# In each quarter, the two down products are put ahead of the product that counts choices

## The reference

```python
h = _L0_tok_ref(x, ...)                                   # 8 x 1024 tokens, 512 wide
h = h + _L0_attn_ref(_layernorm(h), ...)                  # 16 heads, causal, distance decay
h = h + _L0_ffn_ref(_layernorm(h), ...)
# in _L0_ffn_ref:
logits = h @ gate_w.T
scores = jnp.sqrt(jax.nn.softplus(logits))
_, topk_idx = jax.lax.top_k(scores + bias[None, :], K)    # K = 6 of 32
topk_w = take(scores, topk_idx); topk_w = 1.5 * topk_w / topk_w.sum(-1)
pos = (cumsum(onehot(topk_idx)) - 1)[topk_idx]            # place in the expert's list, CAP 192
valid = pos < CAP
y = expert(xb)[eid, pos] * w_slot                         # routed part
si = clip(silu(h @ sg.T) * (h @ su.T), -10, 10)
shared = si @ sd.T                                        # shared expert, all tokens
return routed + shared
```

## Time and profile before

| what | us |
|---|---|
| median of 3 runs | 4119.98 |
| lowest and highest of them | 4116.23, 4120.33 |
| the profiled execution, device time | 4117.86 |
| its span in the trace | 4116.0 |
| mean granted clock of TensorE in it, share of full | 0.881 |

### The profile page before, as it was taken

How to read it: one execution, slowest core, us unless ns; L and a number is a source line. 1 busy time by engine, 2 the same in 40 slices (tenths; PEclk the granted TensorE clock), 3 DMA queues, 4 the chain that set the end, 5 groups by cost and what they waited for, 6 DMA issues and landing times. The chain is left out here.

```text
span 4116.0 us, 62979 instructions
## 1 busy us (share of the span) xinstructions
PE 3420.5 (83%) x20360; PEld 1701.3 (41%) x20360; DVE 2504.0 (61%) x6671; ACT 1041.2 (25%) x2427; POOL 1668.7 (41%) x932
## 2 busy tenths in 40 slices
PE   4776569998888998888898989898988987754998
PEld 1222234444444444444444444444444443233776
DVE  3555424655766577567656765776677576643654
ACT  1111103332332233222223322332333222211111
POOL 3223203543544455345444544454455344522233
PEclk6555589999999999999999999999999998876999
DMA  4444210001111110100011010001000100102996
GB/s 155 151 142 170 111 69 1 27 19 34 73 49 65 45 37 12 47 17 32 22 42 42 11 37 27 32 12 42 22 32 11 50 13 21 45 28 78 263 257 162
DMA packets 123186, 257.65 MB, mean 63 GB/s; under 512 B 38988, under 2 KB 39628, under 8 KB 120192
## 3 DMA queue, kind: packets, MB, share of 16 engines
q1 hardware_dynamic: 78832, 204.56, 14.9%
q0 software_dynamic: 44048, 49.26, 4.7%
HBM read 146.71 MB, written 204.26 MB: 85 GB/s over the span
## 5 line engine op out<-in xcount | busy, mean ns | idle before, releaser
L711 POOL TENSOR_TENSOR a_first_probs<-a_first_probs,a_probs 128x2048 f32<-128x2048 f32 (+3 forms) x320 | 1033.2, 3229 | 1595.5 <-ACT a_probs L773 1376.0
L895 DVE CUSTOM_DVE_ANT_0 a_unused<-a_ps_ring,a_decay 128x512 bf16<-128x512 f32 (+3 forms) x1536 | 774.9, 554 | 518.5 <-PE a_ps_ring L1185 510.5
L773 ACT ACTIVATE a_probs<-a_ps_ring 128x512 f32<-128x512 f32 (+3 forms) x1280 | 505.0, 473 | 795.0 <-PE a_ps_ring L1219 600.4
L715 POOL DMA_INDIRECT d_slots<-a_rows,a_place_i x397 | 394.5, 994 | 249.5 <-DVE a_place_i L1047 141.9
L1209 PE MATMUL a_ps_ring<-a_k_t,a_q_t 32*128 32x512 f32 (+3 forms) x3072 | 413.8, 540 | 67.8 <-DVE a_row_max L895 43.5
L1185 PE MATMUL a_ps_ring<-a_q_t,a_k_t 32*128 32x512 f32 (+3 forms) x3072 | 389.4, 541 | 17.3 <-DVE a_row_max L895 12.4
L1281 PE MATMUL a_ps_dense<-a_sd,a_inner_t 128*128 128x512 f32 x256 | 185.2, 863 | 189.4 <-DVE a_gate_up L1027 186.1
L1173 PE MATMUL a_ps_dense<-a_normed_t,a_q_w 128*128 128x512 f32 x512 | 243.4, 619 | 45.0 <-DMA a_normed_t<-d_normed_t 42.4
L1232 PE MATMUL a_ps_heads<-a_probs,a_values 128*32 128x512 f32 (+3 forms) x2560 | 272.4, 500 | 0.0
L1209 PEld LDWEIGHTS a_ps_ring<-a_k_t,a_q_t 32*128 32x128 f32 x3072 | 146.3, 186 | 270.5 <-issue 142.9
L773 ACT ACTIVATE a_first_probs<-a_ps_ring 128x512 f32<-128x512 f32 x256 | 135.6, 604 | 473.2 <-PE a_ps_ring L1219 448.3
(11 more groups left out here) (169 smaller groups left out, 4575.4 us busy)
## 6 DMA issues: line engine op xcount, KB each, us to landing
d_hidden<-e_hidden SPq DMA_DIRECT2D x8, 2048.0 KB, 7.4
d_normed_t<-e_normed_t SPq DMA_DIRECT2D x8, 2048.0 KB, 11.7
a_normed_t<-d_normed_t SPq DMA_DIRECT2D x8, 2048.0 KB, 7.9
a_residual<-d_hidden SPq DMA_DIRECT2D x64, 256.0 KB, 2.7
d_hidden<-a_residual SPq DMA_DIRECT2D x64, 256.0 KB, 2.0
a_hidden<-d_hidden SPq DMA_DIRECT2D x64, 256.0 KB, 2.7
out<-a_hidden SPq DMA_DIRECT2D x64, 256.0 KB, 2.0
x_w_gate<-w_gate SPq DMA_DIRECT2D x32, 512.0 KB, 6.5
```

The lines of the kernel that those rows point to most:

```text
L711: nc.gpsimd.tensor_tensor(total_of, total_of, probs_of(m)[:, :, 0:width], ALU.add).then_inc(added, 1)
L715: nc.gpsimd.indirect_dma_start(slot_rows, bass.IndirectOffsetOnAxis(ap=place_i[p][:, j, choice:choice + 1], axis=0), rows[p][:, j, :], Non ...
L773: nc.scalar.activation(probs_of(m)[:, h, 0:width], score_bank(m, h)[:, 0:width], ACT.Exp).then_inc(exp_done, 1)
L895: nc.vector.tensor_tensor_reduce(unused[:, h, 0:width], row_bank(k, h)[:, 0:width], decay[:, at:at + width], 1.0, NEG, ALU.add, ALU.max, r ...
```

## The change

Two down products of a quarter stand ahead of its place product: down 0 in slot 10 gap C, where place was, down 1 in slot 11 gap A, where down 0 was, and place in slot 11 gap C, where down 1 was. In the epilogue the same table gives PE's order, and the calls of DVE are swapped to match.

```diff
 QUARTER_AT = ((("turn", 0), 4, A), (("turn", 1), 4, B), (("route", 0), 5, C), (("up", 0), 6, C), (("up", 1), 8, C),
-              (("place", 0), 10, C), (("down", 0), 11, A), (("down", 1), 11, C))
+              (("down", 0), 10, C), (("down", 1), 11, A), (("place", 0), 11, C))
...
                 gate(x, 1, epilogue_use(q, "up", 1), chain)
-                find_places(q % 2, epilogue_use(q, "place", 0), chain)
                 for j in range(2):
                     add_shared(j, epilogue_use(q, "down", j))
+                find_places(q % 2, epilogue_use(q, "place", 0), chain)
```

## The result

| what | before | after |
|---|---|---|
| median, us | 4118.1 | 4192.1 |
| lowest and highest | 4107.97, 4120.33 | 4188.84, 4192.69 |
| the profiled execution, device time | 4117.86 | 4191.54 |
| its span | 4116.0 | 4189.7 |

The changed kernel is slower: ratio 1.0182, with a 95% interval of 1.016 to 1.0204. The prediction was 4164, with a range of 4128 to 4202. Of the four runs of after one was disturbed (4499.96): it is counted in the median of 4192.1, which is 4191.5 without it, and neither in the lowest and highest nor in the ratio.

The account below looks back on a forecast made before the run. PE's time was taken as set by DVE's gate up to down 0, then by PE's own work. Quarters +27.7, epilogue +6.2 and clock +10 made +44 on 4117.86, plus 2.1 for the median: 4164, range 4128 to 4202.

Parts of the forecast that it names:

- The two savings: Ahead of down 0: -0.47 without the wait for L1027, and -1.21 in 26 quarters by L919 falling to 0.29.
- the first saving: Down 0 waits only for inner_done, no longer for L1027: -0.47 us a quarter.
- rival 2: L919 ahead of gate stays at 1.5, POOL's addition not being its cause: 31 us come back, 4195; chance 0.12.
- What was added: Start of down 0 to end of scores(0): 11.6 against 8.99, +2.6; with both savings an ordinary quarter +0.9.
- the split: At scores(0), PE does two heads, waits about 0.2 for row_maxima(11), then does the rest: 1.6 with fourth, shift and mask.
- g = 1: Quarter whose next step lacks a dense product in slot 0: wait of 0.2 and split at scores(1), +1.9 in all.
- g = 3: Quarter before the next entry: scores(0) comes 0.97 late anyway, which covers the wait: -0.1.
- second falls: Clock falling again among slot 0 and 1's small products: one quarter in three, +10, between -3 and +45.
- Rival 1: The clock falls again in every quarter, +45 for the clock: 4199; chance 0.13.
- Rival 3: Clock back before down 0, which takes 1.9 not 3.7: 2.2 saved in 26 quarters, 57 in all, 4107; chance 0.07.
- The last four quarters in steps: Of these the last two were put at +2.4 (no saving on L919) and +0.9 (no next step's row scores).
- The epilogue: Three quarters gain 0.46 each; in the last, L1047 and the scatters come 7.6 later: +6.2 in all.

Follow-up runs that it names:

- e2: Kernel before, with POOL's addition L711 of slot 11 made to wait for inner_done so it can't run beside L919: 4093.41, ratio 0.9946.
- e9: Changed kernel with two more useless matmuls of down's shape right ahead of the place product in steps: 4176.14, ratio 1.0135.
- e3: Changed kernel with four more useless matmuls of down's shape right ahead of the place product in steps: 4195.5, ratio 1.0195.
- e1: Changed kernel with place moved between scores(11) and row_scores(11), and down 1 back in front of the next step's scores(0): 4130.95, ratio 1.0042.
- e10: Kernel before in all its steps, with only the epilogue's four quarters in the new order (down 0, down 1, place): 4119.96, ratio 0.9999.
- e5: Changed kernel with six more useless matmuls of down's shape in the wait ahead of down 0: 4134.64, ratio 1.0055.
- e7: Changed kernel with place between scores(11) and row_scores(11), down 1 before scores(0), and six useless matmuls in the wait ahead of down 0: 4077.2, ratio 0.9904.
- e6: Changed kernel with DVE's division of slot 10 behind gate's last step instead of ahead of it: 4143.63, ratio 1.0074.
- e8: Changed kernel with place before row_scores(11), down 1 before scores(0), slot 10's division behind gate, five useless matmuls in down 0's wait: 4040.72, ratio 0.9824.
- e11: Changed kernel with place before row_scores(11), down 1 before scores(0), DVE's division of slot 10 behind gate, no useless work: 4085.47, ratio 0.9929.

## Why the prediction was right and wrong

The direction and the mechanism in a quarter were right, and the time was inside the range; it missed by 28 us. By the estimates of the table the clock cost 53 us and not 10. That the miss is only 28 is in part luck: the rest of the change cost 26 and not 34, and the first quarter happened to come 5.6 earlier.

**The two savings.** The wait on L1027 is gone, and L919 takes 0.29. Down 0 starts 0.05 behind L1062 in after, so the first saving was 0.55 and not 0.47. e2 shows the second by itself, so rival 2 (L919 stays at 1.5) is out. The Trainium skill, "SBUF — State Buffer", section "SBUF: two separate sides", has DVE and GpSimd take the shared ports by an exclusive lock, a DVE operation with two SBUF inputs among them. e2 agrees: the operation beside the addition is slow, whichever it is (L919 1.50 and then 0.29, the old L1029 0.22 and then 1.13). That whoever starts first keeps the ports does not agree with the earlier trace rows, where L919 starts 0.05 before L711 and is the one that waits.

**What was added.** 11.45 for a predicted 11.6, with the wait of 0.31 and the split where they were forecast; for g = 1 the split at `scores(1)` is there too, but the wait ahead of it is put down to ACT (L773) and not to L895. Over 24 quarters the part of the loss that isn't the clock is 66.3 - 48 = 18 by the estimate of the table, for a predicted 12 x 0.9 + 6 x 1.9 - 6 x 0.1 = 21.6. Inside it two steps were off and cancelled: g = 1 was -0.3 in most and not +1.9, g = 0 and g = 2 were +0.5 and not +0.9, and g = 3 was about +1 to +2.6 and not -0.1. Of g = 1 part is the estimate's doing: in the one quarter whose fall came later (16 us behind L1062) it is +1.4, and in the others the slow PE no longer waits the 0.49 that it waited before. The error at g = 3 was a wrong reading of the earlier trace rows, and that row was the longest of five besides. I took the 0.97 of idle time for the lateness of `scores(0)`, but it was only what down 1 left of an edge of the loop that takes 2 to 4 us: 1.9 of down 1 and 0.17 to 0.97, then 3.03 to 3.44 bare, then 1.98 and 0.93 to 1.78 (e9), then 3.70 and mostly nothing (e3).

**The clock, the step that failed.** I put second falls at one in three quarters and 1.7 us each, +10 (by these two numbers it would be +12). They came in two of three (16 of 24), with 3 to 10 us of busy PE at half speed in each: 93.9 - 6.5 = 87.4 us, which cost some 44 by the estimate of the table, and the first falls 4 more. Both the number and the length were too low, because I sized the term by the one fall in the earlier trace rows behind a wait of 0.49, and did not count with about 3 us of idle time at the edge of the loop, where five of the falls are. Rival 1 (a fall in every quarter, 4199) was nearer to the measured time than the forecast, but not by its own count: it had more falls, each as short as the one in the earlier trace rows.

e1, e3 and e9 show that the missing dense product makes the second falls in the stretch: put back, or replaced by useless products in the same place, they go from 12 to 0, 0 and 6 (in all from 16 to 1, 0 and 8), more than the two by which the kernel before and e10 differ. The four of slot 8 are not explained by it.

The Trainium skill, "TensorE: Matmul & The Clock Gate", section "A second HAM failure mode: psum-queue depth-cycling", tells of a clock that goes up and down where PE idles briefly between groups of matmuls. The trace agrees as far as every one of the 16 has some idle time of PE in the 4 us ahead, though only 0.31 us of it ahead of six. That this wait of 0.31 at `scores(0)` is enough is not borne out: it stands in the quarters with g = 0 and g = 2 too, where the clock fell once in twelve in the stretch, and e9 has five falls with g = 1 without it. At the edge, product and idle time can't be told apart: no run takes the idle time away without putting a product in. Why the clock falls in a quarter with g = 1 and not in one with g = 2, where PE's products from down 0 up to that moment are the same, stays open.

**The clock ahead of down 0.** Rival 3 (the clock is back before down 0) is out: down 0 takes 3.78 behind one unbroken wait of 6.7. The 2.2 a quarter that it put on this is real, though: e5 and e7 get it, 57 and 54 us.

**The last four quarters in steps.** +9.8 for a predicted 6.1, again by the clock, which is low for 23.9 us in one stretch at 3485. Such a stretch is in e1 and e6 too, and not in the kernel before, but e2 has one as well (at 3443, 23.9 us), with the products in the old order. So it is not shown that the change makes it, and its cause stays open.

**The epilogue.** Three quarters gave 3.2 and not 1.4, 2.5 of it by the clock, and the last one cost 6.4 and not 7.6. Alone (e10) the two can't be told from nothing.

## What to carry to other kernels

A dense product that seems to wait in the wrong place may be the one that keeps TensorE's clock up and covers a loop's edge; before it is moved, ask what is left between its neighbours, and size a clock term by how often and how long it can fall, not by the shortest fall seen. A difference of a few tenths in a wait is cheap next to that: here some 18 us by the order and 48 by the clock, or nearer 26 and 40 if the estimate is too high by as much as in e5. Where an engine waits several microseconds anyway, look at what stands ahead of the awaited operation on its own engine: 1.2 us of division behind `gate` instead of ahead of it gave 36 to 48 us in 28 quarters (e6 to after, e8 to e7, e11 to e1).

## What the runs showed of the hardware

- The clock can fall among small products though PE is busy 3.3 to 3.7 of the 4 us ahead: in after 7 times in 24 quarters, for 3.4 to 10.2 us each. A dense product of 1.9 us put into the same stretch halved all its falls (12 to 6), and one of 3.7 us ended them.
- A wait of 6.7 us ahead of a dense product costs 54 to 57 us in 28 quarters by the clock, 2 us each, and useless matmuls in the wait take this back (e5, where some of the 57 is shorter second falls, and e7).
- The edge of the loop takes 2 to 4 us on PE's side, 3.0 to 3.4 when bare, with nothing in the profile to wait for; work issued ahead of it hides it. At all five bare edges of after the clock fell during or right behind it.
- A DVE operation with two operands in SBUF that meets POOL's addition of 1.3 us takes 0.9 to 1.2 us longer, in one case even though it starts first by 0.05 us.
